# Attention and a quantised linear layer on one core: GpSimd's transfers of a half all issued ahead of its adds, other tile pairs, one row transfer, sums at units 19 and 51, the last step rebuilt

## What is computed

```python
def _L0_cond_ref(x, mask, Wq, Wk, Wv, b):        # x (8, 512, 1024), 16 heads of 32
    Q, K, V = (proj(Wq), proj(Wk), proj(Wv))
    att = jnp.einsum('bhqd,bhkd->bhqk', Q, K) * (1.0 / math.sqrt(Dh))
    att = att + b[0]
    m = mask[:, None, None, :]
    att = att * m + (1.0 - m) * NEG_INF
    att = jax.nn.softmax(att, axis=-1)
    y = jnp.einsum('bhqk,bhkd->bhqd', att, V)
...
def _L0_ffn_ref(x, weight, w_scale, bias):       # rows quantised to int8
    q, in_scale = per_token_quant_int8(x)
    acc = jnp.einsum('bsk,nk->bsn', q, weight, preferred_element_type=jnp.int32)
    out = acc.astype(jnp.float32) * in_scale * w_scale[:, 0] + bias
    return out.astype(jnp.float16)
x = x + _L0_ffn_ref(_L0_cond_ref(x, cond_2048, ...), ...)
```

## Time and profile before

| | |
|---|---|
| median of 3 runs | 2414.33 us (2413.55 to 2414.71) |
| profiled execution, its own time | 2414.74 us |
| its span on the core | 2412.8 us |
| first and last block of scores | 557.2 us, 2381.2 us |
| PE busy | 2342.3 us, 97% |
| POOL busy (with its DMA issues) | 1725.1 us, 71% |
| DMA engines busy, 640 to 2300 us | 0.89 |

### The profile page before, as it was taken

The page is one execution under the profiler, slowest core; times in us unless marked ns, Lnnn a source line. Parts: engine busy times, 40 slices in busy tenths (PEclk is TensorE's granted clock), DMA queues, the critical chain, the costliest instruction groups (busy, mean ns, idle before and its releaser), DMA issues.

```text
span 2412.8 us, 36511 instructions
## 1 busy us (share of the span) xinstructions
PE 2342.3 (97%) x11840; PEld 1320.4 (55%) x11872; DVE 1561.4 (65%) x1683; ACT 1343.3 (56%) x2536; POOL 1725.1 (71%) x740
## 2 busy tenths in 40 slices
PE   8999999999999999999999999999999999999996
PEld 7888888885444444444444444444444444444442
DVE  3311111147787777777787877777778777787771
ACT  3322222215666666666666666666666666666664
POOL 3322233324888888888888888888888888888887
PEclk9999999999999999999999999999999999999998
DMA  6645554467888888898988998888988888989971
GB/s 244 255 187 216 200 200 184 175 213 165 194 185 194 193 191 199 195 195 196 203 194 191 195 194 193 190 188 191 196 195 184 197 190 195 201 193 194 204 151 47
DMA packets 152569, 462.60 MB, mean 192 GB/s; under 512 B 15592, under 2 KB 51432, under 8 KB 128304
## 3 DMA queue, kind: packets, MB, share of 16 engines
q0 software_dynamic: 27216, 198.19, 42.9%
q10 hardware_dynamic: 48864, 129.19, 20.5%
q1 hardware_dynamic: 76416, 134.34, 15.5%
HBM read 161.51 MB, written 100.93 MB: 109 GB/s over the span
## 4 chain that ended last, share of the span: by engine, by line
PE 77%; DMA 10%; POOL 5%; issue 3%; ACT 2%; ACTq 1%; SPq 1%; DVE 1%; POOLq 0%; DVEq 0%
PE score L725 18%; PE pv L754 16%; PE ring L131 15%; PE ring L324 11%; PE score L324 9%; DMA q_stack<-max_lo 8%; PE ring L788 4%; POOL acc L1026 4%; PE pv L324 3%; PE ring L769 1%; ACT probs L836 1%; DMA k_stack<-bias_part 1%; ACTq L119 1%; DMA probs<-probs 1%; PE ring L779 1%
## 5 line engine op out<-in xcount | busy, mean ns | idle before, releaser
L836 ACT ACTIVATE probs<-score 128x512 f32<-128x512 f32 x2048 | 1076.8, 604 | 590.6 <-PE score L725 539.8
L140 DVE TENSOR_REDUCE neg_max<-ring 128x1 f32<-128x1024 f32 x1024 | 1210.8, 1220 | 260.3 <-PE ring L131 251.8
L725 PE MATMUL score<-q_stack,k_stack 100*128 100x512 f32 x2048 | 878.1, 430 | 36.4 <-DMA q_stack<-max_lo 21.1
L1026 POOL TENSOR_TENSOR acc<-acc,probs 128x2048 f32<-128x2048 f32 x189 | 876.8, 4639 | 21.5 <-DMA probs<-probs 12.9
L131 PE MATMUL ring<-k_stack,q_stack 98*128 98x512 f32 x2048 | 811.4, 396 | 2.8 <-DMA k_stack<-bias_part 1.8
L725 PEld LDWEIGHTS score<-q_stack,k_stack 100*128 100x128 f32 x2048 | 386.1, 189 | 530.1 <-ACT probs L836 370.9
L754 PE MATMUL pv<-probs,v_in 128*32 128x512 f32 x4096 | 546.3, 605 | 0.0
L131 PEld LDWEIGHTS ring<-k_stack,q_stack 98*128 98x128 f32 x2048 | 389.3, 190 | 73.4 <-DVE neg_max L140 6.8
L1026 POOL TENSOR_TENSOR acc<-probs 128x2048 f32<-128x2048 f32 x63 | 288.7, 4582 | 191.5 <-DMA probs<-probs 121.9
L526 POOL TENSOR_TENSOR q_stack<-x_raw,k_stack 128x1024 fp32r<-128x1024 f32 x28 | 67.7, 2455 | 292.2 <-ACT k_stack L402 292.2
L1010 POOL DMA_DIRECT2D probs<-probs x189 | 172.8, 914 | 52.2 <-PE pv L754 48.8
(11 more groups left out here) (101 smaller groups left out, 1950.0 us busy)
## 6 DMA issues: line engine op xcount, KB each, us to landing
probs<-probs POOLq DMA_DIRECT2D x189, 1024.0 KB, 9.1
q_stack<-qk_part ACTq DMA_DIRECT2D x183, 256.0 KB, 7.9
k_stack<-qk_part ACTq DMA_DIRECT2D x90, 512.0 KB
qk_part<-part_hi SPq DMA_DIRECT2D x64, 512.0 KB, 2.6
qk_part<-part_lo SPq DMA_DIRECT2D x64, 512.0 KB, 3.5
v_steps<-v_out SPq DMA_DIRECT2D x64, 256.0 KB, 2.2
v_out<-x ACTq DMA_DIRECT2D x32, 512.0 KB, 5.6
out<-v_out SPq DMA_DIRECT2D x64, 256.0 KB, 2.0
```

What stands on the lines that cost most here:

```text
L140: nc.vector.tensor_reduce(neg_max[:, pair // CHUNK, pair % CHUNK:pair % CHUNK + 1], ring[:, :], AX_X, ALU.max, negate=True).then_inc(neg_m ...
L725: pe.matmul(score[score_bank(t)][:, :], k_stack[par][0:ROWS, h, kt * P:(kt + 1) * P], q_stack[par][0:ROWS, half, h, :], start=True, stop=T ...
L836: nc.scalar.activation(probs[:, kt, h, :], score[score_bank(t)][:, :], ACT.Exp).then_inc(exp_done, 1)
L1026: nc.gpsimd.tensor_tensor(acc[:, half, :, :], first, probs[:, tile, :, :], ALU.add).then_inc(acc_done, 1)
```

## The change

It does six things. (1) The pairs are tiles 0 into 1, 3 into 2 and 5 into 4 (before: 0 into 1, 2 into 3, 6 into 5), and the first add takes tiles 1 and 2, both of which hold the result of a transfer, where it took tile 4 (no transfer) and tile 1. (2) POOL's order within a step is other: the three transfers of a half are issued ahead of all its adds. (3) The row maxima are doubled by ACT (`double_max`), so that one transfer writes both rows. (4) `sum_rows` stands after units 19 and 51 and `turn_max` after 23 and 55, each alone; the quantised product stands at 43 and 47. (5) The loads of V, the residual and the bias go from ACT's queue to SP's, the K and Q loads to other units, and rounding is done in two instructions of 1024 columns where it was four of 512. (6) In the last step the sums of the second half are made by PE from `probs`, and the steps after them by DVE. The core of the diff:

```diff
-PAIRS_OF_TILES = ((0, 1), (2, 3), (6, 5))
-FIRST, ADDED = 4, (1, 3, 7, 5)
+PAIRS_OF_TILES = ((0, 1), (3, 2), (5, 4))
+FIRST, ADDED = 1, (2, 6, 4, 7)
...
-SUMS_1, TURN_Q, FFN, SUMS_0 = 23, 47, 51, 55
+SUMS_1, TURN_1, TURN_Q, FFN, SUMS_0, TURN_0 = 19, 23, 43, 47, 51, 55
...
+LOAD_K, LOAD_Q1, LOAD_Q0 = (0, 3, 7), (33, 36, 38), (41, 43, 45)
+ROUND, INTS = 31, 39
...
+def double_max(nc, act, neg_max, s, chunk, neg_max_done, doubled):
+
+    act.wait_ge(neg_max_done, PAIRS * s + CHUNK * (chunk + 1))
+    nc.scalar.activation(neg_max[:, chunk, CHUNK:2 * CHUNK], neg_max[:, chunk, 0:CHUNK], ACT.Copy).then_inc(doubled, 1)
...
-def store_max(sp, q_stack, max_hi, max_lo, par, chunk, max_rows):
-
-    for part, rows in ((0, max_hi), (1, max_lo)):
-        dst = q_stack[par][ROW_MAX + part:ROW_MAX + part + 1, chunk, :, :]
-        sp.dma_start(dst.bitcast(F32), rows[:, chunk, :].bitcast(F32)).then_inc(max_rows[chunk], 16)
+def store_max(sp, q_stack, max_parts, par, chunk, max_rows):
+
+    dst = q_stack[par][ROW_MAX:ROW_MAX + 2, chunk, :, :]
+    sp.dma_start(dst.bitcast(F32), max_parts[:, chunk, :].bitcast(F32)).then_inc(max_rows[chunk], 16)
...
+                if ahead and not first:
+                    sp.wait_ge(score_done, UNITS * s + GH + 1)
+                    for part in range(2):
+                        load_bias(sp, bias_d, k_stack, s + 1, 1 - par, part, k_loaded)
+                if not isinstance(s, int) or s >= 2:
+                    store_out(s - 2, 1)
+                    sp.wait_ge(out_stored, 32 * (s - 1))
...
+                sp.wait_ge(max_lo_done, 2 * s + 2)
+                store_max(sp, q_stack, max_parts, par, 1, max_rows)
...
+                    if not ahead and t == UNITS - 1:
+                        last_sums = take_ring(STEPS, STEPS % 2, ("extra", SUMS_1))
+                        sum_tile(4, last_sums, start=True)
+                        sum_tile(5, last_sums)
+                        sum_tile(1, last_sums)
+                        sum_tile(6, last_sums)
+                        weigh(s, par, QH * TT - 1)
+                        sum_tile(7, last_sums)
+                        sum_tile(2, last_sums, stop=True)
...
                 if k == 0:
-                    pool.wait_ge(exp_done, UNITS * s + GH * (half * TT + FIRST + 1))
+                    pool.wait_ge(pair_done[SUMMED_BY[FIRST]], 16 * (halves_before(s, half) + 1))
                     wait(pool, sum_done, halves_before(s, half) - 1)
...
+            def step(s, par, prev=True, ahead=True):
+                if prev:
+                    for k in range(1, ADDS):
+                        add(s - 1, 1, k)
+                begin_pair(s, 0, 0)
                 if prev:
                     normalise(s - 1, 0)
...
+                begin_pair(s, 0, 1)
+                begin_pair(s, 0, 2)
                 if prev:
                     normalise(s - 1, 1)
...
+                for k in range(ADDS):
+                    add(s, 0, k)
+                    if not ahead and k > 1:
+                        begin_pair(s, 1, k - 2)
+                if ahead:
                     begin_pair(s, 1, 0)
                     begin_pair(s, 1, 1)
...
                 if prev:
                     finish(s - 1, 0)
-                if main and ahead:
+                if ahead:
                     begin_pair(s, 1, 2)
                 if prev:
                     finish(s - 1, 1)
...
+                if ahead:
+                    add(s, 1, 0)
...
             all_steps(pool, step)
+            normalise(LAST, 0)
+            finish(LAST, 0)
```

More of the change, by code:

```diff
@@ L77, in wait, with score_bank, score_before, has_max @@
         eng.wait_ge(sem, value)
-def score_bank(t):
+def score_bank(s, t):
+    if isinstance(s, int) and s == LAST and t > SUMS_1:
+        return (t - SUMS_1 - 1 + SCORES) % (SCORES + 1)
     return (t - (t > SUMS_1)) % SCORES
[L85 to L89, removed]
+def score_before(s, t):
+    earlier = [(i - UNITS, score_bank(None, i)) for i in range(UNITS)] + [(i, score_bank(s, i)) for i in range(t)]
+    used = [i for i, bank in earlier if bank == score_bank(s, t)]
+    return used[-1] if used else None
 def max_of_slot(s, t):
     return (s + 1, (t - OWN) // 2) if t >= OWN else (s, (t + UNITS - OWN) // 2)
-def has_max(t, main, ahead):
-    return main and (ahead or t < OWN)
+def has_max(t, ahead):
+    return ahead or t < OWN
 def load_q(eng, qk_d, q_stack, s, par, half, k, loaded):
@@ L643, in _, with store_out @@
         def _(sp):
[L644 to L648, removed]
-                if ahead:
-                    sp.wait_ge(max_hi_done, 2 * s + 3)
+            def store_out(s, half):
+                sp.wait_ge(res_done, 2 * s + half + 1)
+                sp.dma_start(out[bass.ds(s * P, P), half * N:(half + 1) * N],
+                             res[:, half * N:(half + 1) * N]).then_inc(out_stored, 16)
@@ L651, in step @@
                     sp.wait_ge(max_lo_done, 2 * s + 3)
-                    store_max(sp, q_stack, max_hi, max_lo, 1 - par, 0, max_rows)
+                    store_max(sp, q_stack, max_parts, 1 - par, 0, max_rows)
                 if prev:
[L654 to L657, removed]
+                    store_out(s - 1, 0)
@@ L666, in _ @@
                 load_bias(sp, bias_d, k_stack, 1, 1, part, k_loaded)
[L667 to L673, removed]
-            step(STEPS, 0, main=False, ahead=False)
+            all_steps(sp, step)
+            store_out(LAST - 1, 1)
+            sp.wait_ge(out_stored, 32 * LAST)
+            sp.dma_start(res[:, :], x[LAST * P:STEPS * P, :]).then_inc(res_loaded, 16)
+            store_out(LAST, 0)
+            sp.wait_ge(last_res_done, 1)
+            sp.dma_start(out[LAST * P:STEPS * P, N:2 * N], res[:, N:2 * N]).then_inc(out_stored, 16)
             sp.wait_ge(out_stored, 32 * STEPS)
@@ L890, in step @@
+            def step(s, par, prev=True, ahead=True):
+                for t in range(UNITS):
+                    exps(s, t)
+                    loads(s, par, t, ahead)
                     if t == 3 and prev:
                         take_y(s - 1, 1)
-                    if t == SUMS_1 and main:
-                        high_max(nc, act, ring_of(par, ("extra", SUMS_1))[:, N:2 * N], max_hi, s, 1, maxT_done, max_rows, max_hi_done)
-                    if t == 35 and main:
-                        take_y(s, 0)
@@ L896, in step @@
[L896 to L901 removed]
+                    if t == TURN_1 - 2:
+                        double_max(nc, act, neg_max, s, 1, neg_max_done, doubled)
@@ L903, in _ @@
+                    if t == TURN_0 and ahead:
+                        high_max(nc, act, ring_of(par, ("extra", TURN_0)), max_parts, marks, s + 1, 0, maxT_done, max_rows, max_hi_done)
             for i in range(2):
                 act.wait_ge(part_stored[i], 16 * B * STAGES)
-            for s in range(STEPS + 1):
-                step(s, s % 2, prev=s > 0, main=0 <= s < STEPS, ahead=s < STEPS - 1)
+            for s in range(STEPS):
+                step(s, s % 2, prev=s > 0, ahead=s < LAST)
@@ L1026, in add @@
                 nc.gpsimd.tensor_tensor(acc[:, half, :, :], first, probs[:, tile, :, :], ALU.add).then_inc(acc_done, 1)
-            def add_last(k):
-                s, half = STEPS - 1, 1
-                pool.wait_ge(exp_done, UNITS * s + GH * (half * TT + k + 1))
-                if k == 1:
-                    wait(pool, sum_done, halves_before(s, half) - 1)
-                    first = probs[:, 0, :, :]
-                else:
-                    pool.wait_ge(acc_done, ADDS * halves_before(s, half) + k - 1)
-                    first = acc[:, half, :, :]
-                nc.gpsimd.tensor_tensor(acc[:, half, :, :], first, probs[:, k, :, :], ALU.add).then_inc(acc_done, 1)
             def normalise(s, half):
@@ L1085, in step @@
                     finish(s - 1, 1)
-                if main and ahead:
-                    for k in range(1, 3):
-                        add(s, 1, k)
+                if ahead:
+                    add(s, 1, 0)
             all_steps(pool, step)
+            normalise(LAST, 0)
+            finish(LAST, 0)
 def program(nc, x, mask, wqT, wkT, wvT, cond_b, wT, w_scale, f_bias, out):
```

286 lines of the change are left out of this document (157 added, 129 removed).

## The result

The changed kernel takes **2717.2 us** (median of four runs, 2715.5 to 2718.7) against 2414.5 us for the kernel before (four runs, 2413.6 to 2415.9): a ratio of 1.125, with a 95% interval of 1.123 to 1.127. The forecast was 2529 us, at most 2590. The direction was right; of the 303 us that were lost it had forecast 115.

The account below looks back on a forecast made before the run. POOL's loop becomes the bound at 61.2 us a step (adds 37.2 plus two 12.0 waits), above PE's 55.7. First mark 618.5 plus thirty loops gives 2454.5; the last step brings the forecast to 2529 us, range 2500 to 2590.

Parts of the forecast that it names:

- What bounds the kernel before: Whole step before the change: PE sets the pace, 57.28 us a step, at best 55.7 without its visible idle time.
- POOL's loop: POOL's step after the change: eight adds, 37.2 us, plus two open waits of 12.0 for pairs, 61.2 us; chance 0.80.
- The other edits, costed at nothing: Row transfer, doubling, moved loads and earlier sums: no cost while POOL is the bound, at most 1.6 us a step gained.
- without that cover: PE's sums, four units earlier: without POOL's next 12 us wait as cover, a late sum would cost PE all its lateness.
- the rows come late too: Turned rows land behind all three pairs, 17 us after the first; 1.5 to 2 us more a step, 2583 us; chance 0.13.
- The weight of the rule: DMA queues: engines take queues in turn, packet by packet, so rows would overtake the third pair; no size given.
- the row of 6.2 to 6.6 us: Profile row: 8 KB row transfers issued while a pair was under way took 6.2 to 6.6 us, most of a pair's time.
- The sum: Whole run: first mark, thirty loops of 61.2 us, then the last step; span 2527.3 us, forecast 2529.
- The first mark: End of the first add of the second half in step 0, put at 618.5 us.
- The last step: From PE's last sum to the end: 24.8 us before, 5.5 taken off, 19.3 left.
- What the profile would show: Profile after: product every 61.2 us, POOL waiting twice a step, chain alternating adds and pairs, PE's row wait testing late rows.
- The range: Whole run: 2500 us, the forecast's low end, to 2590, just over the late-rows case.

Follow-up runs that it names:

- the best version: Changed kernel with the old GpSimd order and pairs, old places of sums and turned maxima, and two row transfers: 2387.3 us, 0.989 of the kernel before.
- the slowest kernel: Changed kernel with the third pair of each half issued behind that half's first add: 2820.7 us, ratio 1.169 to the kernel before.

## Why the prediction was right and wrong

**What bounds the kernel before.** Confirmed. PE sets the pace; the best version that I ran comes to 56.6 us a step against the 55.7 that PE needs.

**POOL's loop.** Confirmed by size, in the run without the wait for rows: 61.4 to 61.8 us measured, 61.2 forecast; 12.4 in the mean from the first issue to the first add, 12.0 forecast. The second pair did not overlap with the first. It costs about 130 us (2561.5 with the new order, 2431.7 with the old, both with two row transfers), where the forecast gave it all of its 115. But in the kernel after this loop is not the bound. POOL is held up by PE at both ends: 4.18 us for tile 4, then 0.77 for the first pair of the next half.

**The other edits, costed at nothing.** This is the step that failed. "One row transfer for two ... can take away PE's 0.6 us for rows" was wrong in its sign: in this order the one transfer adds 5.0 us a step. In GpSimd's old order it did no harm, and the wait for rows went as the sentence says, from 0.6 us a step to less than 0.2. I had looked at how many transfers there were and at their place in SP's queue, and not at how many engines one of them uses. The sums four units earlier cost nothing in the kernel after, as forecast: the distances between the starts of its scores, in mean over 28 steps, are longer than before by 5.6 us at unit 32, 2.5 in the five units behind it and 1.8 at unit 0; all the others together, those with the sums and turned maxima among them, come to 0.1. Only in GpSimd's old order, without the cover of a 12 us wait, do the old places win 44 us (2431.7 to 2387.3), 1.5 a step. About 1.0 of these is the late sum that "without that cover" warned of: with the new places PE waits 25.8 us in 27 steps for that add, at unit 19. The rest the forecast did not have: in that run PE also takes 1.1 us longer than before from the start of unit 24 to that of unit 25, behind the lone turned maxima, while other distances get shorter.

**The rival that came true** is "the rows come late too", which had 0.13. What it said would be seen came true: the rows landed 1257.2 - 1238.3 = 18.9 us after the first issue (17 said), and PE stopped for 5.1 us at unit 32 (5 said; 7.2 in the longest case). Its reason was half right, since the queue of three pairs is not enough: with the same three pairs ahead, two row transfers landed after 4.9 to 7.2 us. Its price was too small: 1.5 to 2 us a step, for 5.9 measured (67.1 less 61.2). I had looked only for what PE's lateness does to POOL's loop, and left out to add up PE's own. PE needs 56.6 us a step in the best version. In the kernel after the waits for rows of both halves come on top, 211.0 / 27 = 7.8, and 2.5 us at half the clock behind the longer one: 66.9, and 67.1 are measured. In the run with two row transfers the same sum is 56.6 + 99.3 / 26 = 60.4, and 1.3 for the clock at the two stretches behind the waits: 61.7, level with the 61.4 to 61.8 of POOL's loop. That is why taking the wait away as well won only 4 us. So beside POOL's loop PE has a slack of some 5 us in a step, and lateness of up to that is free; the single row transfer brought 10.

**The weight of the rule.** I said that by packet-by-packet arbitration "the rows would overtake the third pair and this rival falls", and that the row of 6.2 to 6.6 us "speaks only half for it". The row was the better witness: with one piece on each of 16 engines it already took 6 us beside a pair. I never counted the pieces, one on each of 16 engines before, 16 on each of two after.

**The sum.** The first mark, 618.5 us, was met within 2: in the kernel after that add ends at 1.9 us later (615.91 + 4.52). The 30 steps took 67.1 us each and not 61.2, 177 us more. From the last mark, at 2633.9 us, to PE's last sum were 63.7 us for 53.5 forecast, another 10. By the runs, the 303 us are 156 for the form of the row transfer, 130 for GpSimd's order and pairs and 17 for the rest (undone in this order; with GpSimd's order put back first it is 284 for that and 2 for the form), in which the places of sums and turned maxima lose 44 and the other edits win 28. The last step: forecast 19.3 us from PE's last sum to the end. In the timeline of the kernel after,

```profile
2697.71 0.72 DVE L964 STREAM_TRANSPOSE sums_turned<-ring 128x512 f32<-128x512 f32 x1 [4.12 <-PE ring L816]
```

it is 2716.2 - 2697.6 = 18.6. From the last score to the end it took 31.6 us before and takes 25.9, so 5.7 less, with 5.5 forecast.

**What the profile would show.** The product every 61.2 us: 67.2. POOL's waits: about 4 us for PE and 2 for the pair in one half, almost all for PE in the other. POOL busy about 50 us a step: 49. The chain between adds and pairs: no, between PE and the rows. PE's wait at unit 32: there, and decisive.

**The range** ended at 2590 because the rival's price was the only thing that I let stretch it. A resource that a new form of transfer uses, for which no row of before stood, should have been bounded from above by its slowest case.

## What to carry to other kernels

Before merging small transfers, look at the outer dimension of the merged one: two rows on two engines, each behind a neighbour's big packets, took 10.5 to 12.8 us where two transfers took 5 to 7. When bulk transfers are issued back to back, ask which small, urgent transfer falls behind them and who waits for it; a harmless form (2 us in one order) cost 156 us in another. And when a lateness is to vanish in another engine's slack, write out the loop of each engine: the slack is there only if the engine that has it is not itself the one that is late.

## What the runs showed of the hardware that I had not expected

After 5.1 us of idleness PE was granted half its clock (0.50, matmuls of 0.63 us in place of 0.39) for its first 5.7 us of work, and such stretches add 2.5 us a step to the wait itself. A shorter stop can bring it too: after the 1.7 us before unit 0 in this step, matmuls took 0.62 us and more from 1225.5 to 1228.9 us, though the first six behind the stop ran at full clock. In the whole run the mean clock fell from 0.995 before to 0.944, and to 0.916 in the slowest kernel. And none of the rows' 512-byte pieces moved in the first 4.6 us after the issue, while the pair before it was moving, nor any of the two transfers' in their first 3.7; what holds them back for that long I did not settle.
